# The next block's token transposes in front of the second gate-and-up half

## What is computed

```
gate_logits = einsum('bsd,de->bse', x, gate_kernel)
top_k_weights, top_k_indices = top_k(gate_logits, 2)
top_k_weights = softmax(top_k_weights)
h0 = einsum('bsd,edm->bsem', x, w0_kernel)      # 256 -> 512, per expert
h1 = einsum('bsd,edm->bsem', x, w1_kernel)
inter = silu(h0) * h1
out = einsum('bse,bsem,emd->bsd', combine, inter, wo_kernel)   # 512 -> 256
```

## Time and profile before

| | us |
|---|---|
| median of 3 runs | 809.29 (806.13 to 809.66) |
| the profiled execution | 808.83 |
| its span, first to last instruction | 807.0 |

### The profile page before, as it was taken

The page is one execution under the profiler, slowest core; times in us unless marked ns, Lnnn a source line. Parts: engine busy times, 40 slices in busy tenths (PEclk is TensorE's granted clock), DMA queues, the critical chain, the costliest instruction groups (busy, mean ns, idle before and its releaser), DMA issues.

```text
span 807.0 us, 19409 instructions
## 1 busy us (share of the span) xinstructions
PE 756.3 (94%) x5952; PEld 643.5 (80%) x5952; DVE 512.3 (63%) x2117; ACT 480.5 (60%) x1537; POOL 424.3 (53%) x674
## 2 busy tenths in 40 slices
PE   3789999999999999999999999998798999999994
PEld 3678898888888889888888888876587778888883
DVE  5688676767757757766775785888665754333331
ACT  2477877776777777777777767768455432222221
POOL 1365665655655556556565555555324545554442
PEclk9999999999999999999999999999999999999998
DMA  6433123303212130231221213025962233222330
GB/s 204 122 108 105 58 64 73 73 32 76 67 34 61 47 75 33 69 71 35 73 67 38 57 41 76 31 66 152 387 208 40 43 51 50 46 39 43 52 52 6
DMA packets 52852, 61.05 MB, mean 76 GB/s; under 512 B 10545, under 2 KB 45617, under 8 KB 52753
## 3 DMA queue, kind: packets, MB, share of 16 engines
q1 hardware_dynamic: 45264, 50.46, 21.3%
q0 software_dynamic: 7488, 9.36, 6.9%
HBM read 26.21 MB, written 9.32 MB: 44 GB/s over the span
## 4 chain that ended last, share of the span: by engine, by line
PE 78%; DVE 11%; ACT 4%; issue 4%; DMA 1%; SPq 1%; POOLq 0%; POOL 0%; DVEq 0%; ACTq 0%
PE h L1610 13%; PE projected L379 10%; PE attn_out L526 10%; PE probsT L486 9%; PE scores L473 9%; PE yb L1629 8%; PE heads_out L505 6%; PE projected L400 3%; PE heads_out L508 3%; PE projected L357 2%; PE tg L1620 2%; ACT exps L601 1%; ACT exps L599 1%; DMA raw<-w_attn 1%; DVE masked L726 1%
## 5 line engine op out<-in xcount | busy, mean ns | idle before, releaser
L976 POOL TENSOR_SCALAR probs<-exps,inv_sums 128x128 f32<-128x128 f32 x256 | 97.3, 380 | 216.9 <-DVE inv_sums L734 169.7
L608 ACT COPY pT<-probsT 128x384 f32<-128x384 f32 x256 | 121.8, 476 | 82.5 <-PE probsT L486 82.4
L599 ACT ACTIVATE exps<-masked,neg_max 128x128 f32<-128x128 f32 x256 | 103.0, 402 | 54.4 <-DVE neg_max L728 54.2
L486 PE MATMUL probsT<-identity,probs 128*128 128x128 f32 x768 | 130.6, 279 | 5.0 <-ACT pT L608 4.8
L601 ACT ACTIVATE exps<-masked,neg_max 128x256 f32<-128x256 f32 x256 | 127.3, 497 | 0.0
L977 POOL TENSOR_SCALAR probs<-exps,inv_sums 128x256 f32<-128x256 f32 x256 | 125.7, 491 | 0.0
L1832 POOL DMA_INDIRECT out<-y,to_token x39 | 61.9, 1587 | 107.4 <-DVE y L1751 85.2
L379 PE MATMUL projected<-xT_hi,w 128*128 128x256 f32 x512 | 113.6, 302 | 4.9 <-DVE k_sin L716 2.5
L1610 PE MATMUL h<-experts_w,xsT_hi 128*128 x312 | 106.8, 424 | 2.3 <-DVE xsT_lo L1741 1.3
L728 DVE CUSTOM_DVE_ANT_0 masked<-scores,tables 128x256 f32<-128x256 f32 x256 | 107.4, 419 | 0.2 <-issue 0.2
L473 PE MATMUL scores<-kT,qT 64*128 64x128 f32 (+1 forms) x1024 | 102.9, 341 | 2.7 <-DMA qT<-rotated 2.7
(11 more groups left out here) (181 smaller groups left out, 1626.3 us busy)
## 6 DMA issues: line engine op xcount, KB each, us to landing
qT<-rotated SPq DMA_DIRECT2D x256, 64.0 KB, 2.2
kT<-k_cos SPq DMA_DIRECT2D x64, 128.0 KB, 3.4
experts_w<-w_in SPq DMA_DIRECT2D x16, 512.0 KB, 7.0
raw<-w_attn SPq DMA_DIRECT2D x20, 256.0 KB, 3.3
experts_w_out<-w_out SPq DMA_DIRECT2D x8, 512.0 KB, 7.7
out<-x_all SPq DMA_DIRECT2D x8, 256.0 KB, 2.3
xn_rows<-raw SPq DMA_DIRECT2D x8, 256.0 KB, 3.9
x_all<-x SPq DMA_DIRECT2D x1, 1792.0 KB, 10.5
```

Source lines behind the costliest of these rows:

```text
L486: mm = nc.tensor.transpose(p_bank[:, at:at + P], probs[:, h, at:at + P], ident[:, :])
L599: nc.scalar.activation(exps[:, h, 0:P], masked[:, h, 0:P], ACT.Exp, bias=neg_max[:, h, 0:1], scale=-1.0, accum_out=sums[:, h, 0:1])
L608: nc.scalar.copy(pT[:, n % 2, h, :], p_bank[:, 0:3 * P]).then_inc(pT_done, 1)
L976: nc.gpsimd.tensor_scalar(probs[:, h, 0:P], exps[:, h, 0:P], inv_sums[:, h, 0:1], 1.0, ALU.mult, ALU.mult)
```

## The change

In the loop of PE's stream, and in the piece ahead of it for block 0, the call of `x_transposes` for the next block moves from behind the second half to a place in front of it. Nothing else in the kernel differs.

```diff
         hidden(0, expert, 0)
+        x_transposes(1)
         hidden(0, expert, 1)
-        x_transposes(1)
 
         for j in range(1, BLOCKS):
...
             hidden(j, expert, 0)
             g_transposes(j - 1)
-            hidden(j, expert, 1)
             if j < LAST:
                 x_transposes(j + 1)
+            hidden(j, expert, 1)
             outputs_ready(j - 1)
             output(j - 1, last)
```

## The result

| | before | after |
|---|---|---|
| median, us | 810.26 (8 runs, 806.13 to 812.45) | 814.32 (8 runs, 811.84 to 815.12) |
| ratio, 95% interval | | 1.0044 [1.0027, 1.0062] |
| profiled execution, us | 808.83 | 814.67 |
| its span, us | 807.0 | 812.7 |
| expert stage of the profiled execution, us | 206.98 | 210.66 |

The changed kernel is slower by 4.06 us between the medians, and the interval of the ratio does not contain 1. By the bound of 0.5% that the prediction set it is still "the same", by a hair: 0.44% by the ratio of the table.

The account below looks back on a forecast made before the run. It took TensorE as the expert stage's bound, 5.17 us a block. Terms 4.1 (block 13 late) + 1.0 + 0.9 + 0.4 = 6.4 us, added to the three-run median, gave 815.7; range 810.5 to 819.5.

Parts of the forecast that it names:

- first rival: Waits for gathers fall into time idle anyway, or are short: 3.4 us more, 812.7, or down to 810.5; chance 0.20.
- block 6 begins: After block 5's stall, register loads come out behind the output product, so block 6 starts 0.4 late.
- the second half 0.22 later in its block: Transposes now run ahead of the second half, so it ends 0.22 later in every block, and `x_lo` with it.
- rings, blocks 6 to 12: Gather ring from `gate_rows` to the next lengthens by 1.63, 1.49 and 1.33 over three turns: 4.45 us together.
- block 12 gives back: TensorE's 0.76 standstill before the output product, and the transposes' 0.22 now behind it, return 0.95.
- blocks 13 to 16: Between block 13's start, put 4.1 late, and the wait in block 16, no further loss was counted.
- block 16: The gather of block 17's tokens lands after the transposes' new, earlier place: a wait of 1.0.
- price one, late blocks: From block 15 on, the later `x_lo` delays each next first half by 0.03 to 0.04: 0.9 us.
- late gathers: After block 16, some three gathers landing late cost 0.4 together, between 0 and 1.0.
- the earlier copy frees nobody: ScalarE's earlier copy of transposed tokens gains nothing, because `x_lo` follows `gate_rows` on VectorE, which waits for the second half.
- Block 5: A 1.6 wait before it is swallowed: the product begins 1.6 later but at 2.4 GHz ends as before.
- The rival of a gain: Transposes' gather wait moves where more work covers register loads: up to 7.0 faster, 802.3; chance 0.05.

Follow-up runs that it names:

- Experiments 1 to 4: Against the kernel before: new order in late blocks alone 1.0004, in early blocks alone 1.0045; four gathered-row buffers with new order 0.9990, with old order 0.9995.
- experiment 6: Changed kernel with ScalarE's copy of the tokens held longer after the second half, by four spare copies of 36 columns; 821.97 us, ratio 1.0154 to the kernel before.
- experiment 5: Changed kernel with ScalarE's copy of the tokens held until the second half has ended, behind one small spare copy; 815.44 us, ratio 1.0064 to the kernel before.
- experiment 1: Kernel before, with the transposes moved early only from iteration 18 on; 810.44 us, ratio 1.0004.
- experiment 3: Changed kernel with four buffers for gathered rows instead of three, and two for the lo parts; 809.70 us, ratio 0.9990 to the kernel before.
- experiment 4: Kernel before (old order) with four buffers for gathered rows instead of three, and two for the lo parts; 809.88 us, ratio 0.9995.

## Why the prediction was right, and where it was off

The direction and the mechanism held: slower, through gathers that the transposes now reach too early, in blocks whose ring has no slack. Experiments 1 to 4 show it. The size was 6.4 us as forecast and 3.68 in the stage (4.06 between the medians), the low end of the forecast's own range and nearer to the 3.4 of its first rival. That the time itself came within 1.4 is in part luck: the forecast was added to a median of three runs, 809.29, and the eight runs of the kernel before have 810.26. So 814.32 lies above the 813.3 up to which the prediction called a time the same, while the ratio of 1.0044 is below its 0.5%, on the side to which it had given 0.20. Two of its signs fell short as well: of the distances between `gate_rows` only the first reached 12.4, and block 13 began 2.17 late instead of about 4. Term by term:

| step of the prediction | predicted | measured |
|---|---|---|
| block 6 begins | +0.4 | -0.66 |
| the second half 0.22 later in its block | +0.2 | +0.22 |
| rings, blocks 6 to 12 | +4.45 | +3.56 |
| block 12 gives back | -0.95 | -0.95 |
| blocks 13 to 16 | 0 | -0.12 |
| block 16 | +1.0 | +0.88 |
| price one, late blocks | +0.9 | 0 |
| late gathers | +0.4 | +0.75 |
| sum | 6.4 | 3.68 |

The measured terms are the shifts of single block starts and of `gate_rows`, taken one after the other. That block 12 gave back just what was forecast is partly chance. The output product there was also quicker by 0.26, 1.99 before and 1.73 after. The other way, `gate_rows` of block 12 had come 0.33 behind its half in the kernel before, where it waited for silu (its releaser in the earlier trace rows), and came 0.09 behind it after the change:

```profile
655.24 1.99 PE yb L1629 x8
...
659.67 1.73 PE yb L1629 x8
```

**The step that failed: "the earlier copy frees nobody".** It read `x_lo` as held by `gate_rows`, because `gate_rows` stands in front of it in VectorE's order and ended just before. The copy's end was as near, and with 0.21 from one engine to the other it was the copy that came last. Once it comes before the second half ends, `x_lo` ends 1.20 after that half instead of 1.35, in every kernel of the table that has the new order in its late blocks, no held copy and VectorE's old order (1.35 in each with the old order), and the 0.9 of price one falls to 0. The limit itself was right: the prediction had `x_lo` at 1.35 cost 0.03 to 0.04 a block, and experiment 6 puts the free limit at 1.30. It was the position of `x_lo` that was wrong, and with it the signpost that late blocks would take 5.2 with `x_lo` as what ends the wait.

**The rings were the right step with a term too large.** The tail from late transposes to the next `gate_rows` was put at 1.93 and measured 1.95, 1.93 and 1.92. What was too long was the rest, taken over unchanged from the earlier trace rows: from `gate_rows` to the transposes' load it is 11.05, 10.13 and 10.04, not 11.17, 10.49 and 10.46. Of the 0.9 in all, 0.56 is `gate_rows` to the gather's issue; the earlier `x_lo` (0.15 a turn, 0.45) would be most of it, which was not tested by itself. 0.34 is issue to load: GpSimd itself took 0.99, 1.30 and 1.65 for these issues where it had taken 0.99, 1.40 and 1.92, 0.37 less, and why is open.

**Block 5 swallowed more than I let it.** The waits ahead of it moved the output product there by 0.88, not 1.6, and the 0.4 for register loads behind it did not show. The chain of the changed kernel, for the earlier trace rows:

```profile
616.38 0.48 ACT gT L1693
616.87 0.13 issue
617.00 1.99 PE yb L1629 x8
```

The clock stayed up, as taken, though the product took 1.99 and not the 1.73 reckoned with; it was 3.52. Against the start of the stage it ends 0.65 earlier than before.

**The rivals.** That the waits fall into idle time did not happen in the rings: its signs, under 3 us of waits and gates 11 apart, are 9.5 us and 12 to 13. But what it said of block 5 was true there. The rival of a gain was right in one piece: TensorE's "issue" at the first halves fell from 5.2 to 3.8, too little against the gathers. By an estimate from the figures of the Trainium skill (DMA: Bandwidth & Descriptors, Anatomy of one DMA) a gather would land 2.3 us after its issue; in the changed kernel, too, the quickest row is 2.7 and the median 2.8:

```profile
DMA to landing us min/median/max: 2.7/2.8/6.7
```

With that estimate the sum would have been 2.6, and the measured 3.68 lies between that and the forecast; but the row does not bear the estimate out, and of what the forecast had too much only the 0.34 above is time from an issue to a load.

## What to carry to other kernels

Moving a consumer earlier in an in-order engine does not only make it ready earlier: it moves the deadline of the load that feeds it, and everything that stands behind the consumer, here the half on which the next load depends, now waits with it. Ask first whether the buffers of that load form a ring without slack; if so, add a buffer before moving the consumer (the move cost 4 us with three buffers and nothing with four). And to find what releases an instruction that stands behind two nearly simultaneous events, compare distances from each: the right one is at the same distance wherever it comes last (0.21 or 0.22 from the copy in three kernels), the other is not (0.06 after `gate_rows` had ended in the kernel before, 0.02 before that end with the copy held).

## What the runs showed of the hardware that was not expected

**The same code ahead of the stage takes different times.** Over the ten profiled executions the expert stage began between 577.8 and 584.6, although the attention in front of it is the same in all. That is more than the change costs. The stretch of the first 60 us is one place, in the changed kernel and in experiment 5, whose stages began at 583.51 and 577.82 (columns as in the earlier trace rows):

```profile
0.00:60.00 60.00, 38.45 (x261) 32.26 (x262) 42.03 (x161) 28.14 (x83) 22.61 (x37) 0.91 0.49 146
```

```profile
0.00:60.00 60.00, 37.85 (x291) 31.76 (x293) 45.27 (x171) 30.65 (x93) 25.07 (x40) 0.97 0.51 155
```

The granted clock is 0.91 in the one and 0.97 in the other, and about a tenth fewer instructions were through by then. It is not the whole of it: experiment 1 had 0.94 there and began its stage last, at 584.56. What makes the clock fall in one execution and not in another stays open. For a difference of half a per cent, stages have to be compared from their own starts, and the verdict left to many runs.

**The clock in block 5.** After the stall in which TensorE waits for the copy of the gated rows, the output product took 3.52, 3.65 and 3.61 in three profiled executions (before, experiments 1 and 3) and 1.99 in the seven others. It is worth about 1.6 us. In the kernel before TensorE's granted clock went to the lower of its two levels, 1.2 GHz, 0.3 us before that product began. The order of the transposes alone does not decide it: experiment 3, where it fell, has the new order there, and experiment 4, where it did not, the old one. What TensorE did just before is more telling. In the five kernels with three buffers and the new order in early blocks its standstill was in two pieces, 1.1 to 1.6 us for the gather and 0.6 to 0.7 for the copy, and the clock fell in none of them. In the other five it was one piece of 2.0 to 2.4 us, and the clock fell in three. So the prediction's guess that two pieces would leave the clock up agrees with all ten, but with one execution of each kernel it is not shown, and what decided among the five stays open.

**Issuing a gather takes GpSimd between 0.95 and 1.97 us over the ten profiled executions.** In the earlier trace rows it is 0.99, 1.40 and 1.92 in the three ring gathers, in the changed kernel 0.99, 1.30 and 1.65, with the same bytes. Why was not tested.
